# Two-layer transformer on one core: the first layer's maxima turned by one transpose and placed by three DMAs

## The reference, cut to what matters

```python
x = x + L0_attn(layernorm(x))     # 16 heads, three attentions a1, a2, a3
x = x + L0_ffn(layernorm(x))      # spiking feed-forward
x = x + L1_attn(layernorm(x))     # 16 heads of 16 columns, causal
x = x + L1_ffn(layernorm(x))      # sign of the weight

def _attn(q, k, v, causal):
    s = einsum(q, k) * scale
    if causal: s = where(tril, s, min)
    return einsum(softmax(s), v)

# in L0_attn, with the same q (head size 96) for all three:
a1 = _attn(q, k1, v1, causal=True)     # 512 keys
a2 = _attn(q, ks, vs, causal=False)    # 64 selected keys
a3 = _attn(q, kw, vw, causal=True)     # 512 keys
out = (g0 * a1 + g1 * a2 + g2 * a3) @ w_proj
```

## Time and profile before

| | |
|---|---|
| median of 3 runs | 3582.85 us (3581.64 to 3582.94) |
| the profiled execution, its own time | 3588.78 us |
| its span, first to last instruction | 3586.9 us |
| TensorE busy | 3273.3 us (91%), mean granted clock 0.941 |
| VectorE (DVE) busy | 1987.1 us (55%) |
| ScalarE (ACT) busy | 1567.3 us (44%) |
| GpSimd (POOL) busy | 927.5 us (26%) |
| DMA queues | 4.8% of the 16 engines' span |

### The profile page before, as it was taken

How to read it: one execution, slowest core, us unless ns; L and a number is a source line. 1 busy time by engine, 2 the same in 40 slices (tenths; PEclk the granted TensorE clock), 3 DMA queues, 4 the chain that set the end, 5 groups by cost and what they waited for, 6 DMA issues and landing times.

```text
span 3586.9 us, 58807 instructions
## 1 busy us (share of the span) xinstructions
PE 3273.3 (91%) x20560; PEld 2333.5 (65%) x20560; DVE 1987.1 (55%) x6976; ACT 1567.3 (44%) x3441; POOL 927.5 (26%) x1840
## 2 busy tenths in 40 slices
PE   4999789998899979999899998999889998899978
PEld 3676657765677656776567765677656766567665
DVE  3664565555556465554656546566455554566445
ACT  1444344543454334543445525445253542544424
POOL 0222322222222222222222232222322223222222
PEclk7999899998999989999899998999999998999989
DMA  2000000000000000000000000000000000000000
GB/s 80 30 19 7 6 13 25 19 7 1 19 19 19 7 1 25 19 13 7 1 25 19 13 7 1 31 13 13 6 1 31 19 7 6 13 19 19 7 6 7
DMA packets 31438, 53.75 MB, mean 15 GB/s; under 512 B 3472, under 2 KB 13456, under 8 KB 30864
## 3 DMA queue, kind: packets, MB, share of 16 engines
q1 hardware_dynamic: 31120, 49.64, 4.3%
HBM read 44.91 MB, written 4.72 MB: 14 GB/s over the span
## 4 chain that ended last, share of the span: by engine, by line
PE 79%; DVE 11%; issue 4%; POOL 3%; ACT 2%; PEld 1%; PEldq 1%; SPq 0%; DMA 0%; POOLq 0%; ACTq 0%; DVEq 0%
PE outs L896 14%; PE work L820 7%; PE work L781 7%; PE work L857 6%; PE work L802 6%; PE work L858 5%; PE work L859 5%; PE work L903 4%; PE outs L1007 3%; DVE work L1124 3%; PE work L777 3%; PE work L786 2%; PE work L997 2%; PE work L861 2%; PE work L791 2%
## 5 line engine op out<-in xcount | busy, mean ns | idle before, releaser
L1480 ACT ACTIVATE PR<-work 128x512 f32<-128x512 f32 (+1 forms) x1088 | 640.5, 597 | 580.3 <-PE work L859 477.3
L1124 DVE CUSTOM_DVE_ANT_0 work<-work,KEEPB 128x384 f32<-128x384 f32 (+3 forms) x1536 | 665.5, 480 | 75.5 <-PE work L820 74.1
L1606 POOL TENSOR_SCALAR_AFFINE_SELECT PR<-PR 128x256 f32<-128x256 f32 (+1 forms) x960 | 348.3, 366 | 952.5 <-ACT PR L1480 948.6
L1108 DVE TENSOR_TENSOR BIG<-work,BIG 96x512 fp32r<-96x512 f32 (+1 forms) x455 | 285.4, 629 | 355.0 <-ACT BIG L1375 355.0
L820 PE MATMUL work<-BIG 96*128 96x448 f32 (+9 forms) x1664 | 447.9, 367 | 36.6 <-DVE NMX L1124 15.9
L1596 POOL TENSOR_TENSOR TOK<-AB 128x256 f32<-128x256 f32 (+1 forms) x325 | 219.2, 674 | 877.5 <-DVE AB L1078 854.8
L896 PE MATMUL outs<-PR,ONES 128*32 128x512 f32 (+4 forms) x2304 | 404.5, 458 | 0.0
L857 PE MATMUL work<-BIG 99*128 99x512 f32 (+4 forms) x1152 | 404.5, 351 | 0.0
L820 PEld LDWEIGHTS work<-BIG 96*128 96x128 f32 (+1 forms) x1664 | 285.2, 207 | 174.7 <-issue 91.7
L1077 DVE TENSOR_TENSOR AB<-work,COS 128x256 f32<-128x256 f32 (+2 forms) x357 | 150.0, 420 | 426.9 <-PE work L781 366.3
L858 PE MATMUL work<-BIG 96*128 96x512 f32 (+4 forms) x1152 | 382.4, 332 | 0.0
(11 more groups left out here) (161 smaller groups left out, 5280.9 us busy)
## 6 DMA issues: line engine op xcount, KB each, us to landing
WKW<-w_kw_dram SPq DMA_DIRECT2D x65, 256.0 KB, 2.8
WSEL<-w_sel_dram SPq DMA_DIRECT2D x65, 256.0 KB, 3.0
X<-x_dram SPq DMA_DIRECT2D x9, 512.0 KB, 3.4
out_dram<-X SPq DMA_DIRECT2D x9, 512.0 KB, 2.8
WFC<-w_fc_dram SPq DMA_DIRECT2D x1, 1024.0 KB, 9.9
WFP<-w_ffp_dram SPq DMA_DIRECT2D x1, 1024.0 KB, 11.9
WQKV<-w_qkv_dram SPq DMA_DIRECT2D x1, 768.0 KB, 13.0
WQ<-w_q_dram SPq DMA_DIRECT2D x1, 576.0 KB, 7.4
```

The lines of the kernel that those rows point to most:

```text
L1108: read_work(v.tensor_tensor(dst[1], src, dst[0].bitcast(F32), ALU.subtract), use)
L1124: last = v.tensor_tensor_reduce(ps[:, lo:hi], ps[:, lo:hi], KEEPB[:, T - (hi - lo):T], -1.0, -NEG, ALU.add, ALU.min, dst)
L1480: a.activation(PR[0:rows, j % NP, :], ps[0:rows, :], ACT.Exp).then_inc(exp_ready, 1)
L1606: gp.affine_select(blocks, blocks, [[0, len(cols)], [1, P]], ALU.is_ge, 0.0, base=0, channel_multiplier=-1).then_inc(exp_masked, 1)
```

## The change

It turns all 24 columns of NMX by one transpose into 24 rows x 128 of one bank. ScalarE copies these once into a new tile, MROWS (24 rows, two buffers). The sync engine then issues three DMAs, one for each attention, each of 8 rows x 512 B from MROWS into one row of QW, 4 KB long (the copy's order of rows is a, h, tile, so the rows follow each other). The next pair's first unit waits for the three DMAs. Four numbers of `AFTER` move: the pieces by 0.42 units, the maxima by 0.4, mt by 0.57 in all, and tail 0 from -7.2 to -7.8.

```diff
-AFTER = [dict(pv=2.67, tr=1.82, sum=0.75, group=1.98, piece=-2.58, gap=0.66, piece_tr=2.36, max=4.9, max_gap=0.31,
-              mt=2.12, rows=-5.38, tail=[(-7.2, -7.15), (-4.0, -5.2), (-2.4, -3.9), (-1.5, -2.3)]),
+AFTER = [dict(pv=2.67, tr=1.82, sum=0.75, group=1.98, piece=-3.0, gap=0.66, piece_tr=2.36, max=4.5, max_gap=0.31,
+              mt=1.95, rows=-5.38, tail=[(-7.8, -7.75), (-4.0, -5.2), (-2.4, -3.9), (-1.5, -2.3)]),
...
-            if s[0] == "mt" and layer == 0:
-                for h in range(2):
-                    work.use((0,) + s + (h,))
-            elif s[0] in ("unit", "max", "mt", "out_tr", "group"):
-                work.use((layer,) + s, {"unit": 0, "mt": 2}.get(s[0], 1))
+            if s[0] in ("unit", "max", "mt", "out_tr", "group"):
+                work.use((layer,) + s, {"unit": 0, "mt": 1 + layer}.get(s[0], 1))
...
+        MROWS = sb("MROWS", [24, 2, P], F32R)
...
+        MAXIMA_PLACED = 16 * 3
...
+            def place_maxima(p):
+                was_read(sp, work, work_read, (0, "mt", p))
+                for a in range(3):
+                    sp.dma_start(QW[p % 2][0][D0 + a:D0 + a + 1, 0:2, :].bitcast(F32),
+                                 MROWS[8 * a:8 * a + 8, p % 2, :].bitcast(F32)).then_inc(maxima_placed, 16)
...
+                    elif s[0] == "mt_out":
+                        place_maxima(s[1])
...
-                    for h in range(2):
-                        ps, done = take((0, "mt", p, h), W)
-                        for t in range(NT):
-                            c = h * NT + t
-                            last = nc.tensor.transpose(ps[0:3, t * P:(t + 1) * P], NMX[:, p % 2, c:24:8], ID[:, :])
-                        last.then_inc(done, 1)
+                    ps, done = take((0, "mt", p), W)
+                    nc.tensor.transpose(ps[0:24, 0:P], NMX[:, p % 2, :], ID[:, :]).then_inc(done, 1)
...
-                    for use in maxima_uses(layer, p):
-                        was_read(pe, work, work_read, use)
+                    if layer == 0:
+                        pe.wait_ge(maxima_placed, MAXIMA_PLACED * (p + 1))
+                    else:
+                        was_read(pe, work, work_read, (1, "mt", p))
...
             def maxima_out(layer, p):
-                for h in range(2):
-                    if layer == 0:
-                        ps = full(act, (0, "mt", p, h), WORK)
-                        read_work(copy(QW[p % 2][0][D0:D0 + 3, h, :], ps[0:3, :]), (0, "mt", p, h))
-                    else:
...
+                ps = full(act, (layer, "mt", p), WORK)
+                if layer == 0:
+                    if p >= 2:
+                        act.wait_ge(maxima_placed, MAXIMA_PLACED * (p - 1))
+                    read_work(copy(MROWS[:, p % 2, :], ps[0:24, 0:P]), (0, "mt", p))
+                    return
```

More of the change, by code:

```diff
@@ L497, in build_program @@
         max_ready = sem("max_ready")
+        maxima_placed = sem("maxima_placed")
         exp_ready = sem("exp_ready")
@@ L531, in build_program @@
         WORK = (work, work_full, WB)
-        def maxima_uses(layer, p):
-            return [(0, "mt", p, 0), (0, "mt", p, 1)] if layer == 0 else [(1, "mt", p)]
+        MAXIMA_PLACED = 16 * 3
         def end_pass(e, n):
@@ L1113, in maxima @@
                 if i == 0 and layer * NPAIR + p >= 2:
-                    full(dve, maxima_uses(*((layer, p - 2) if p >= 2 else (0, NPAIR - 2 + p)))[-1], WORK)
+                    full(dve, (layer, "mt", p - 2) if p >= 2 else (0, "mt", NPAIR - 2 + p), WORK)
                 for n, (lo, hi, att, h, qt) in enumerate(u["segs"]):
@@ L1446, in maxima_out @@
             def maxima_out(layer, p):
-                for h in range(2):
-                    if layer == 0:
-                        ps = full(act, (0, "mt", p, h), WORK)
-                        read_work(copy(QW[p % 2][0][D0:D0 + 3, h, :], ps[0:3, :]), (0, "mt", p, h))
-                    else:
-                        ps = full(act, (1, "mt", p), WORK)
-                        read_work(a.activation(QZ[2 * D1:2 * D1 + 2, p, h, :], ps[0:2, :], ACT.Copy,
-                                               scale=ID[0:2, h:h + 1]), (1, "mt", p))
+                ps = full(act, (layer, "mt", p), WORK)
[4 more added lines that the diff above has]
+                    return
+                for h in range(2):
+                    read_work(a.activation(QZ[2 * D1:2 * D1 + 2, p, h, :], ps[0:2, :], ACT.Copy,
+                                           scale=ID[0:2, h:h + 1]), (1, "mt", p))
             def outputs(layer, n, att):
```

## The result

The changed kernel takes 3600.57 us (3595.28 to 3601.93), the kernel before, beside it, 3582.89 (3581.22 to 3587.74): ratio 1.0045, with a 95% interval of 1.0032 to 1.0058. Slower by 18 us. I had forecast 3566, with a range to 3590, and had given slower 0.2. The prediction was wrong.

What follows compares the result with a forecast made beforehand. TensorE, busy without a hole, was taken to bound the kernel. Transposes -48.7, first-pair order +2.4, stops +15.2 and +3.6, clock +9, with resuming, gave -17 us: 3566 us as a median, range 3549 to 3590.

Steps and rivals of the forecast that it cites:

- seven transposes less: On TensorE in each of 64 pairs, seven of eight transposes go, 0.109 us each: 0.76 us a pair, 48.7 us saved.
- order of the list: Reordered steps cost nothing in pairs between; in the first pair, later HN transposes cost 0.3 us, 2.4 us in all.
- last pair's stop: Before the last pair's unit 0, TensorE waits 1.9 us for the DMAs, 15.2 us over eight sequences.
- first pair's stop: Before the first pair's unit 0, TensorE waits 0.45 us for the DMAs, 3.6 us over eight sequences.
- resuming behind the stops: TensorE takes an estimated 0.1 us to resume behind each of the 16 stops.
- clock behind the last stop: TensorE's clock falls to half behind the last pair's stop in 3 of 8 sequences, 3 us each: 9 us.
- sign of being wrong: The forecast is wrong if a pair shrinks by clearly less than 0.7 us.
- What moves: In pairs between, reordered steps nearly balance in changes between kinds of work: 0, bounds 0.1 us a pair, 6 us.
- The chain of the last pair: From the transpose through ScalarE's copy, three DMA issues and landing to unit 0: 4.55 us, landing 1.5.
- Pairs between: DMAs stay hidden: 6.3 us of cover from mt to unit 0 against 4.55, so 1.75 us to spare.
- rival 3: Slower by the last pair's stop (2.8 us), first stop 1.35, clock falls in all sequences: +11, 3594 us; chance 0.14.
- threshold of 5.8: The kernel gets slower once stops and lost clock exceed 5.8 us a sequence.

Runs made afterwards that it cites:

- e3: Changed kernel, but first and last pair of each sequence by the eight transposes and two copies of before; 3562.70 us, ratio 0.9928 to the kernel before.
- e1: Changed kernel's order alone, with eight transposes and two copies in all pairs and no DMAs; 3599.01 us, ratio 1.0029 to the kernel before.
- e7: Changed kernel with one list number altered, so the additions and store stand ahead of piece 1 again; 3600.34 us, ratio 1.0043 to the kernel before.
- e8: Changed kernel plus eight transposes in pair 4 that nobody reads; 3616.16 us, ratio 1.0090 to the kernel before.
- e11: Changed kernel with the last pair alone by eight transposes; 3572.07 us, ratio 0.9953 to the kernel before.
- e10: Changed kernel with one DMA of 12 KB for all 24 rows in place of three of 4 KB; 3569.07 us, ratio 0.9945 to the kernel before.
- e9: Kernel before, only mt moved, ahead of unit 10, by one transpose and DMAs in six pairs between; others eight transposes; 3545.68 us, ratio 0.9890.

## Why the prediction was wrong

Per sequence, with the runs' numbers (times 8 for the kernel). The last two rows ahead of the sum count the whole span, the first sequence and both ends of the run with it, so they differ a little from the means above:

| step | predicted | measured |
|---|---|---|
| seven transposes less, 8 pairs | -6.1 | -6.1 (e3: 0.76 a pair) |
| order of the list | +0.3 | +1.67 (e1) |
| last pair's stop | +1.9 | +2.16 (27.35 - 25.96 + 0.77) |
| first pair's stop | +0.45 | +1.45 |
| resuming behind the stops | +0.2 | in the two above |
| clock behind the last stop | +1.1 | +1.3, +1.4 (two executions) |
| all other stretches | 0 | +1.2, +0.5 |
| sum | -2.1 | +1.7, +1.1 |

Times 8 this is 13 and 9 us. The spans of the two profiled executions, 3600.0 and 3594.7, lie 13.1 and 7.8 above the 3586.9 before; the medians say 18 and 10.

- *The transposes*: right in cause and size, the size with some luck. Eight take 0.80 us ahead of a unit and the one that stays 0.03, where I had 0.87 and 0.11. A pair of the changed kernel takes 30.63 us, with TensorE busy throughout; 30.5 was forecast. That is 0.60 to 0.63 less than before in the means, short of the 0.7 that I had named as a sign of being wrong, and the order is what lies between.
- *What moves, "I take 0, with bounds of 0.1 us a pair"*: this step failed. The order costs 0.14 to 0.21 us in a pair between. Counting kinds of neighbours says nothing of what a change between them costs. Both prices of a piece's start stood in the trace of before: 0.33 us behind a unit, and 0.43 directly behind the four L786, as in the first pair there:

```profile
547.53 0.59 PE L777 MATMUL work<-WQ,NQT 96*128 96x192 f32 x2
547.96 1.03 PE L781 MATMUL work<-WKW,HT 128*128 128x256 f32 x4
```

- *The first pair*: this step failed too, and for a reason that could have been read. I priced HN's transposes (2.4 us) and the DMAs' chain, and took the store's data to be moved before the DMAs start. The store hangs on step tail 3, which the list now has behind piece 1. So VectorE's additions come late, TensorE waits 0.69 us for them, and the sync queue issues the store at 987.92 and the three DMAs only from 988.38, though MROWS had been ready at 987.06:

```profile
986.35 1.27 DVE L1278 TENSOR_TENSOR X<-X,work 128x512 f32<-128x512 f32 x2
...
986.81 0.25 ACT L1379 ACTIVATE MROWS<-work 24x128 fp32r<-24x128 f32 x1
...
987.92 0.41 SPq L609 DMA_DIRECT2D out_dram<-X  x1
988.38 2.07 SPq L614 DMA_DIRECT2D BIG<-MROWS  x3
```

I had walked the order of the sync queue by its names before (store ahead of mt_out), not by the times at which its releasers now come. e7 puts the store back and splits the 1.0 us by which the stop of 1.45 exceeds the 0.45 forecast: 0.52 is the late issue, and 0.48 stays, which is the chain's own terms of the next item. What I did price, the transposes of HN at 0.3 us, was 0.07.
- *The chain of the last pair*: the mechanism was right, the terms were off in both directions. First issue at T + 1.78 (predicted 2.23), issues 0.69 apart (predicted 0.4, from loads whose issue took 0.33 and 0.43), third at T + 3.15 (3.03), landing 1.80 (1.5, bounds 1.2 and 2.4), unit 0 at T + 4.95 (4.55). The last pair stops 2.28 us for a forecast 1.9. The fixed part of about 2.0 us in the Trainium skill (DMA: Bandwidth & Descriptors, Anatomy of one DMA), fitted there on GpSimd's path, would have been nearer than my 1.5.
- *Pairs between*: hidden, as forecast, with 6.27 us against a chain of 4.95 (1.75 us to spare forecast, 1.3 left).
- *The clock*: 9 us forecast behind the stops, three falls of 3 us. In the two executions of the changed kernel 11 and 11 us, in two and three falls of 1.6 to 6 us each. That this came so near is luck: behind the same stop e7 lost 25 us and e8 27.
- *Rivals*: rival 3, the last pair's stop, named the right place and nearly the time (3594). e11 shows that this place alone decides the sign, and e10 that its length does. But its price of all bounds at once was not needed: stops of 3.7 us and 1.3 us of lost clock, 5.0 together, stayed below its threshold of 5.8, and the order made up the rest.

**Open.** Why the same stop of 2.28 us is followed by a fall in two to eight of eight sequences isn't settled, nor why P to mt and M to P of the changed kernel were together 1.5 us longer in one execution and 0.7 in the other (means of the stages table), while in the ten other kernels they lie between -0.4 and +0.3 us of the kernel before. They differ by where the low clock lies in them. A tie between the length of a sequence and the falls, tested by e8, predicts those stretches and not the time. Which changes between neighbours make the order's 1.0 us in the pairs between is open too.

## What to carry to other kernels

Cover for a new latency has to be counted at the ends of a loop as well as in its middle: six pairs of eight hid these DMAs, the two others made a gain of 0.7% (e3) into a loss, and leaving them as they were (e9) was the best version. If a step has to come earlier, move that step alone. Where several small DMAs feed one waiter, join them: the issue of each was 0.69 us in the chain, more than the bytes cost.

## What the runs showed of the hardware

- The issue of a DMA of 8 rows x 512 B within the core's memory holds the sync queue for 0.64 us, where the weights' loads of 256 KB take 0.33 and 0.43. One of 24 rows takes 0.73 (median of 64 in e10), so three times the rows cost 0.09 more. From the start of the issue to the waiter's first matmul: 1.80 us for 4 KB, 2.15 for 12 KB.
- Eight transposes of 3 columns of weights take 0.80 us from their start to the next unit's (e3), eight more of 24 columns added 0.85 us (e8), and a single one of 24 ahead of a unit took 0.03.
- The last pair's stop of 1.26 us in an otherwise busy TensorE was followed by a fall of the clock in none of 8 sequences, stops of 2.2 to 2.3 us in 26 of 40, and the loss was up to 6.2 us.
- Two orders of the same matmuls, both without a wait in TensorE's timeline, differed by 0.14 to 0.21 us in a pair of 31.3.
